# Convolution stage: the VectorE tap sums are built in PSUM, ScalarE and GpSimd take over one tap of each convolution, TensorE does two edge taps instead of three

## The reference

```
m = bilinear 32x32 -> 64x64 of mask
q, k, v = 1x1 convolutions of x; attention with 8 heads of 32 over the 4096 positions -> fuse
x = (Wf . [x, fuse] + bf) * m + x * (1 - m)                       # layer 0

edge = relu(bn(dwconv3x3(x, edge_w)))                             # nine taps for each channel
att  = sigmoid(fc2 . relu(fc1 . mean(x)))
out  = bn1(fusion_w . [x * att, edge] + fusion_b)
out  = dwconv3x3(out, deform_w)                                   # nine taps for each channel
out  = bn2(balance_w . out + balance_b)
return out * x                                                    # layer 1
```

## Time and profile before

| | |
|---|---|
| median of 3 executions | 4203.85 us (4203.06 to 4205.12) |
| the profiled execution | 4203.13 us, of which the span from first to last instruction is 4201.3 us |
| TensorE, busy share of the span | 96% |
| VectorE | 84% |
| GpSimd | 77% |
| ScalarE | 56% |
| granted TensorE clock, mean | 0.976 of full speed |

### The profile page before, as it was taken

One profiled execution on the slowest core, in us unless ns is written; L12 is line 12 of the kernel. 1 busy time (PEld: TensorE's weight loads), 2 busy tenths in 40 slices (PEclk: granted clock), 3 DMA queues, 4 the chain that ended last, 5 costly groups with the idle time before them and its releaser, 6 DMA issues. The chain is left out here.

```text
span 4201.3 us, 81722 instructions
## 1 busy us (share of the span) xinstructions
PE 4044.0 (96%) x20341; PEld 1975.3 (47%) x20341; DVE 3550.1 (84%) x5350; ACT 2339.9 (56%) x4424; POOL 3222.2 (77%) x1360
## 2 busy tenths in 40 slices
PE   7979999999999999999999999999999999969797
PEld 4534444444444444444444444444444444424343
DVE  3279999999989999999899999999999999917989
ACT  1216666666656666666566666666666666641213
POOL 2429999999989999999899999999999999960000
PEclk9959999999999999999999999999999999989998
DMA  6931100110001101110111011100110000013021
GB/s 190 285 100 39 41 21 22 42 39 22 21 23 41 31 21 32 41 31 21 31 41 31 21 31 38 35 20 18 40 38 21 21 21 21 17 27 85 20 80 40
DMA packets 213798, 184.92 MB, mean 44 GB/s; under 512 B 115986, under 2 KB 140740, under 8 KB 213316
## 3 DMA queue, kind: packets, MB, share of 16 engines
q1 hardware_dynamic: 213508, 181.74, 16.2%
HBM read 122.10 MB, written 59.24 MB: 43 GB/s over the span
## 5 line engine op out<-in xcount | busy, mean ns | idle before, releaser
L761 ACT ACTIVATE prob<-st 128x512 f32<-128x512 f32 x4096 | 2154.3, 601 | 1309.3 <-PE st L626 1048.6
L819 DVE TENSOR_REDUCE block_max<-mx 128x1 f32<-128x512 f32 x4096 | 2562.0, 683 | 343.4 <-PE mx L633 330.0
L490 POOL TENSOR_TENSOR prob_sum<-prob_sum,prob 128x1024 f32<-128x1024 f32 x768 | 1929.3, 2512 | 127.5 <-POOL prob_sum L490 100.4
L633 PE MATMUL mx<-keys,max_queries 96*128 96x512 f32 x4096 | 1648.0, 426 | 38.2 <-DMA keys<-k_scratch 27.8
L626 PE MATMUL st<-queries,keys 97*128 97x512 f32 x4096 | 1574.5, 411 | 1.6 <-ACT prob L761 1.5
L490 POOL TENSOR_TENSOR prob_sum<-prob 128x1024 f32<-128x1024 f32 x448 | 1067.8, 2383 | 253.1 <-ACT prob L761 253.1
L633 PEld LDWEIGHTS mx<-keys,max_queries 96*128 96x128 f32 x4096 | 777.8, 191 | 737.3 <-DVE block_max L819 564.8
L645 PE MATMUL acc<-prob,values 128*32 128x512 f32 x8192 | 1039.7, 602 | 0.0
L626 PEld LDWEIGHTS st<-queries,keys 97*128 97x128 f32 x4096 | 776.7, 190 | 520.6 <-ACT prob L761 282.2
L645 PEld LDWEIGHTS acc<-prob,values 128*32 128x32 f32 x8192 | 194.4, 108 | 427.1 <-issue 226.1
L665 PE MATMUL dacc<-prob_sum,ones 128*32 128x512 f32 x2048 | 273.0, 605 | 9.2 <-POOL prob_sum L490 9.2
(11 more groups left out here) (119 smaller groups left out, 1213.8 us busy)
## 6 DMA issues: line engine op xcount, KB each, us to landing
max_queries<-q_scratch SPq DMA_DIRECT2D x384, 64.0 KB, 1.9
queries<-q_scratch SPq DMA_DIRECT2D x384, 64.0 KB, 2.0
keys<-k_scratch SPq DMA_DIRECT2D x168, 128.0 KB, 2.5
x<-in_x SPq DMA_DIRECT2D x18, 512.0 KB, 4.1
q_scratch<-high SPq DMA_DIRECT2D x32, 256.0 KB, 4.4
k_scratch<-high SPq DMA_DIRECT2D x16, 512.0 KB, 4.9
q_scratch<-low SPq DMA_DIRECT2D x32, 256.0 KB, 5.0
k_scratch<-low SPq DMA_DIRECT2D x16, 512.0 KB, 4.9
```

What stands on the lines that cost most here:

```text
L490: ops.tensor_tensor(psum[k][:, :, :], a[:, :, :], prob[(first + i) % RING][:, :, :], ALU.add).then_inc(added[own], 1)
L633: nc.tensor.matmul(mx[bank(j, p)][:, :], qm[p][:, h, ns * P:(ns + 1) * P], kk[gp][0:SPLIT, h, blk * CH:(blk + 1) * CH], start=True, stop=T ...
L761: nc.scalar.activation(prob[s % RING][:, h, :], st[bank(i, p)][:, :], ACT.Exp).then_inc(exp_done, 1)
L819: nc.vector.tensor_reduce(bmax[p][:, j // MB, j % MB:j % MB + 1], mx[bank(j, p)][:, :], AX.X, ALU.max).then_inc(mx_taken, 1)
```

## The change

`EDGE_PE` goes from 3 to 2: TensorE does edge taps 0 and 1. VectorE does edge taps 2 to 7, in place in the PSUM tile `back[p][ct]`, and only its last step writes `conv[p]` in SBUF. The deform sum is built in the same way: ScalarE writes tap 0 into `back`, VectorE does taps 1 to 7 there (seven steps where there were eight), the last of them writing `conv`. For both convolutions ScalarE weighs tap 8 into a new SBUF tile `tap[p]` and GpSimd adds it to `conv[p]` (`add_tap`). The consumers of `conv` (`relu` on ScalarE, `balance` on TensorE) wait for GpSimd's sum. Since `back[p]` now holds the deform sum of a chunk as well as its balance product, ScalarE's deform taps wait for `last_ready`, and in ScalarE's order `balanced(c)` stands ahead of `deform_taps(c+2)`.

```
-EDGE_PE = 3
-EDGE_DVE = TAPS - EDGE_PE
-DEFORM_DVE = TAPS - 1
+EDGE_PE = 2
+EDGE_DVE = TAPS - EDGE_PE - 1
+DEFORM_DVE = TAPS - 2
...
+        tap = [sb(f"last_tap{p}", [P, CT, CH]) for p in range(2)]
...
 # TensorE: edges(), balance()
-                pe.wait_ge(edge_step, EARLIER * EDGE_DVE + CT * EDGE_DVE * (n - 2) + CT)
+                pe.wait_ge(edge_step, EDGE_DVE * (EARLIER + CT * (n - 1)))
...
-                pe.wait_ge(deform_step, CT * DEFORM_DVE * (n + 1))
+                pe.wait_ge(tap_added, CT * (deform_round(b, c) + 2))
...
 # ScalarE: relu(), and the taps
-                    act.wait_ge(edge_step, EDGE_DVE * (EARLIER + CT * (b * NCH + c)) + CT * (EDGE_DVE - 1) + ct + 1)
+                    act.wait_ge(tap_added, CT * (edge_round(b, c) + 1) + ct + 1)
...
+            def last_tap(src, weights, c, p, r):
+
+                act.wait_ge(tap_added, CT * r)
+                for ct in range(CT):
+                    nc.scalar.activation(as_rows(tap[p][:, ct, :]), inner(src, ct, c, k=TAPS - 1), ACT.Identity,
+                                         scale=keep[weights][:, ct, TAPS - 1:TAPS]).then_inc(tap_ready, 1)
+
+            def edge_tap(b, c, p, nxt=1):
+                act.wait_ge(y_ready, tile_done(b * NCH + c + nxt, CT - 1))
+                last_tap(y, "etaps", c, p, edge_round(b, c))
+
+            def deform_taps(b, c, p, nxt=1):
 
                 n = b * NCH + c
                 act.wait_ge(o1_ready, tile_done(n + nxt, CT - 1))
-                act.wait_ge(bal_mm, freed(n))
+                act.wait_ge(edge_step, EDGE_DVE * (EARLIER + CT * NCH * (b + 1)))
+                act.wait_ge(last_ready, freed(n))
                 for ct in range(CT):
-                    nc.scalar.activation(as_rows(conv[p][:, ct, :]), inner(o1, ct, c, k=0), ACT.Identity,
-                                         scale=keep["dtaps"][:, ct, 0:1]).then_inc(tap_ready, 1)
+                    nc.scalar.activation(as_rows(back[p][ct][:, :]), inner(o1, ct, c, k=0), ACT.Identity,
+                                         scale=keep["dtaps"][:, ct, 0:1]).then_inc(first_ready, 1)
+                last_tap(o1, "dtaps", c, p, deform_round(b, c))
...
 # ScalarE: order (each relu(c) has edge_tap(c + 1) ahead of it)
                         fused(b, c2 * 2 + p + 3, 1 - p)
-                        first_tap(b, c2 * 2 + p + 2, p)
                         balanced(b, c2 * 2 + p, p, c2)
+                        deform_taps(b, c2 * 2 + p + 2, p)
                 fused(b, NCH - 1, 1)
-                first_tap(b, NCH - 2, 0)
                 balanced(b, NCH - 4, 0, HALF - 2)
-                first_tap(b, NCH - 1, 1, nxt=0)
-                for c in range(NCH - 3, NCH):
+                deform_taps(b, NCH - 2, 0)
+                balanced(b, NCH - 3, 1, HALF - 2)
+                deform_taps(b, NCH - 1, 1, nxt=0)
+                for c in range(NCH - 2, NCH):
                     balanced(b, c, c % 2, c // 2)
...
 # GpSimd
+            def add_tap(p, r, step, done):
+
+                for ct in range(CT):
+                    pool.wait_ge(step, done + ct + 1)
+                    pool.wait_ge(tap_ready, CT * r + ct + 1)
+                    nc.gpsimd.tensor_tensor(conv[p][:, ct, :], conv[p][:, ct, :], tap[p][:, ct, :], ALU.add
+                                            ).then_inc(tap_added, 1)
...
 # VectorE: edges() and deform()
+                        part = as_rows(back[p][ct][:, :])
                         nc.vector.scalar_tensor_tensor(
-                            out=as_rows(conv[p][:, ct, :]), in0=inner(y, ct, c, k=k),
-                            scalar=keep["etaps"][:, ct, k:k + 1],
-                            in1=as_rows(back[p][ct][:, :] if i == 0 else conv[p][:, ct, :]),
+                            out=part if i < EDGE_DVE - 1 else as_rows(conv[p][:, ct, :]), in0=inner(y, ct, c, k=k),
+                            scalar=keep["etaps"][:, ct, k:k + 1], in1=part,
                             op0=ALU.mult, op1=ALU.add).then_inc(edge_step, 1)
...
                 dve.wait_ge(o1_ready, tile_done(n + nxt, CT - 1))
+                dve.wait_ge(edge_ready, tile_done(b * NCH + NCH - 2 + p, CT - 1))
+                dve.wait_ge(bal_mm, freed(n))
```

More of the change, by code:

```diff
@@ L915, in image_phase @@
         edge_step = sem("edge_step")
-        tap_ready = sem("first_tap_ready")
+        first_ready = sem("first_tap_ready")
+        tap_ready = sem("last_tap_ready")
+        tap_added = sem("last_tap_added")
         edge_ready = sem("edge_ready")
@@ L939, in image_phase @@
         tile_done = lambda n, t: EARLIER + CT * n + t + 1
+        edge_round = lambda b, c: 2 * NCH * b + c
+        deform_round = lambda b, c: 2 * NCH * b + NCH + c
         def inner(t, ot, c, rows=ROWS, k=4):
@@ L1118, in fused @@
                                          bias=keep["nshift"][:, 1, ot:ot + 1]).then_inc(o1_ready, 1)
-            def first_tap(b, c, p, nxt=1):
+            def last_tap(src, weights, c, p, r):
[7 more added lines that the diff above has]
+            def deform_taps(b, c, p, nxt=1):
                 n = b * NCH + c
                 act.wait_ge(o1_ready, tile_done(n + nxt, CT - 1))
-                act.wait_ge(bal_mm, freed(n))
+                act.wait_ge(edge_step, EDGE_DVE * (EARLIER + CT * NCH * (b + 1)))
+                act.wait_ge(last_ready, freed(n))
                 for ct in range(CT):
-                    nc.scalar.activation(as_rows(conv[p][:, ct, :]), inner(o1, ct, c, k=0), ACT.Identity,
-                                         scale=keep["dtaps"][:, ct, 0:1]).then_inc(tap_ready, 1)
+                    nc.scalar.activation(as_rows(back[p][ct][:, :]), inner(o1, ct, c, k=0), ACT.Identity,
+                                         scale=keep["dtaps"][:, ct, 0:1]).then_inc(first_ready, 1)
+                last_tap(o1, "dtaps", c, p, deform_round(b, c))
             def balanced(b, c, p, c2):
@@ L1139, in _ @@
                 act.sem_inc(s, EARLIER)
+            act.sem_inc(tap_added, CT)
             with act.Fori(0, B) as b:
+                edge_tap(b, 0, 0)
                 with act.Fori(0, HALF - 2) as c2:
                     for p in range(2):
+                        edge_tap(b, c2 * 2 + p + 1, 1 - p)
                         relu(b, c2 * 2 + p, p)
+                edge_tap(b, NCH - 3, 1)
                 relu(b, NCH - 4, 0)
@@ L1149, in _ @@
                 nc.scalar.activation(nexp[:, :], front[1][1][:, 0:CT], ACT.Exp, scale=-1.0).then_inc(nexp_ready, 1)
+                edge_tap(b, NCH - 2, 0)
                 relu(b, NCH - 3, 1)
+                edge_tap(b, NCH - 1, 1, nxt=0)
                 relu(b, NCH - 2, 0)
@@ L1154, in _ @@
                 fused(b, 1, 1)
-                first_tap(b, 0, 0)
+                deform_taps(b, 0, 0)
                 fused(b, 2, 0)
-                first_tap(b, 1, 1)
+                deform_taps(b, 1, 1)
                 with act.Fori(0, HALF - 2) as c2:
@@ L1174, in _ @@
                     nc.gpsimd.memset(edge_rows, 0.0).then_inc(borders, 1)
+            def add_tap(p, r, step, done):
[4 more added lines that the diff above has]
+                                            ).then_inc(tap_added, 1)
+            with pool.Fori(0, B) as b:
+                with pool.Fori(0, HALF) as c2:
+                    for p in range(2):
+                        c = c2 * 2 + p
+                        add_tap(p, edge_round(b, c), edge_step,
+                                EDGE_DVE * (EARLIER + CT * (b * NCH + c)) + CT * (EDGE_DVE - 1))
+                with pool.Fori(0, HALF) as c2:
+                    for p in range(2):
+                        c = c2 * 2 + p
+                        add_tap(p, deform_round(b, c), deform_step,
+                                CT * DEFORM_DVE * (b * NCH + c) + CT * (DEFORM_DVE - 1))
         @block.vector
@@ L1236, in deform @@
                         if i == 0:
-                            dve.wait_ge(tap_ready, CT * n + ct + 1)
+                            dve.wait_ge(first_ready, CT * n + ct + 1)
                         else:
                             dve.wait_ge(deform_step, base + CT * (i - 1) + ct + 1)
[L1240 to L1243, removed]
+                        part = as_rows(back[p][ct][:, :])
+                        nc.vector.scalar_tensor_tensor(
+                            out=part if i < DEFORM_DVE - 1 else as_rows(conv[p][:, ct, :]), in0=inner(o1, ct, c, k=i + 1),
+                            scalar=keep["dtaps"][:, ct, i + 1:i + 2], in1=part,
+                            op0=ALU.mult, op1=ALU.add).then_inc(deform_step, 1)
             def result(b, c, p):
```

## The result

The changed kernel takes 4233.08 us (median of 4, 4232.05 to 4238.42) beside 4203.45 us before (median of 4): a ratio of 1.0073, 95% interval 1.0055 to 1.0090, so 29.6 us slower. The forecast was 4230, slower.

The account below looks back on a forecast made before the run. TensorE was taken to pace the edge part, VectorE the deform part. 2 x (-4.1 - 5.3) + 7 x 6.0 + 1.2 + 1.9 = +26.3 us on 4203.13 gave 4229.4, for the median 4230; range 4206 to 4252.

Parts of the forecast that it names:

- The wait for the store: Deform loop: `balanced(c)` awaits the store of chunk c-2 ahead of the first tap, leaving VectorE idle 5.4 us a period.
- first reading: Kernel before: ScalarE's 106.4 us in ten waits on the store cost nothing, since VectorE never stands for them.
- The additions against VectorE: GpSimd's additions hold VectorE operations with both inputs in SBUF: result products 1.9 us a chunk, edge `y` 0.6.
- rival 2: Deform and edge parts: the additions don't hold VectorE's products and `y` operations; 23 us less, 4207; chance 8%.
- rival 4: Mainly the edge part: GpSimd also holds steps such as `diff`, because of their pointer scalar; +20 us, about 4250; chance 5%.
- The steps in PSUM: VectorE's edge and deform steps writing PSUM in place keep a spacing of 0.663 us from start to start.
- Rivals 1: VectorE's steps in PSUM don't overlap: +29 us, 4259; chance 14%.
- 3: VectorE's steps are shorter in PSUM: at 0.605 us spacing 20 us less, 4210; chance 9%.
- 5: VectorE's steps: write and read of one PSUM bank take turns, doubling the step; +187 us, 4417; chance 3%.
- rival 6: Deform loop: the chain over the store doesn't form, its wait being met early; 38 us less, 4192; chance 3%.
- The edge part: VectorE becomes the pace at 11.13 us a chunk; with the passage to the deform part, -4.1 us an image.
- The deform part and the end: Deforms 0 to 3 give -5.3 us an image; seven periods cost +6.0 each; image 1's rest +1.2, the end +1.9.

Follow-up runs that it names:

- experiment 3: The changed kernel with GpSimd adding only one of 512 columns of each last tap, all waits kept: 4206.25 us, 1.0010 of the kernel before.
- experiment 1: The changed kernel with `result(c)` ahead of `deform(c+3)` in VectorE's deform loop instead of behind it: 4193.17 us, 0.9978 of the kernel before.
- experiment 2: The changed kernel with four tiles `last` instead of two, VectorE's order kept: 4192.74 us, 0.9980 of the kernel before.
- experiment 5: The changed kernel with `result(c)` after the first two double steps of `deform(c+2)`, for chunks 0 to 5: 4181.88 us, 0.9956 of the kernel before.
- experiment 8: The changed kernel with the deform sum in SBUF (`conv`) and ScalarE's order as before the change: 4219.34 us, 1.0045 of the kernel before.
- experiment 4: The changed kernel with VectorE's sums in SBUF (`conv`), only each chunk's first step reading `back`: 4234.97 us, 1.0078 of the kernel before.
- experiment 6: experiment 5 plus edge steps placed between `diff` and `y` and ahead of the gate's operations: 4177.32 us, 0.9943 of the kernel before.

## Why the prediction was right, step by step

*The wait for the store.* Shown. Seven waits of 5.33 to 5.58 us where 5.4 was taken, and 38 to 40 us go with either of two edits that have only the store's wait in common.

The prediction's first reading went too far, though: it says that the wait costs nothing before the change and that VectorE never stands for it. That holds in the loop. At the passage between the images of the kernel before ScalarE waits 33.43 us for a store, and VectorE's results 6 and 7 wait 7.24 us for ScalarE (ScalarE's timeline, then VectorE's):

```profile
4003.59 2.79 ACT L1134 ACTIVATE last<-back,nshift,nscale 128x512 f32<-128x512 f32 x4 [33.43 <-DMA out_dram<-last]
...
4004.40 2.70 DVE L1248 TENSOR_TENSOR last<-last,y 128x512 f32<-128x512 f32 x4 [7.24 <-ACT last L1134]
```

After the change VectorE waits 7.46 us there, so the sum isn't touched.

*The additions against VectorE.* Shown in place and size: pairs of products of 3.09 to 3.16 us where 1.21 + 1.9 was forecast, `y` of 1.32 to 1.40 for 0.68 (at eleven places; rival 2 counts twelve), and 1.29 again for the products without the additions. `diff`, whose pointer scalar lies in SBUF, isn't held, which settles rival 4 at nothing. The Trainium skill (SBUF — State Buffer, Who interferes with whom) says that a VectorE instruction with two SBUF inputs contends with a GpSimd instruction that reads SBUF, and that one with at most one SBUF input doesn't, outside VectorE's 2-port modes; the trace agrees for these forms, with 3.09 for 1.29 and 1.40 for 1.40.

*The steps in PSUM.* 0.659 from start to start; 744 and 750 ns on average beside 745 and 746. Rivals 1, 3 and 5 fall; rival 2 falls with experiment 3, rival 6 with experiments 1 and 2. The Trainium skill's extra 65 ns for a PSUM source (VectorE: DVE Perf Modes, The TRN2 errata) doesn't show here either: 384 more steps have such a source, and the average of neither group is longer by more than 5 ns.

*The edge part.* The chunk was right (11.10 for 11.13), the stretch gained 2.0 and 2.4 us instead of 4.1. The mis-sized term is the gate, which the sum left out. It runs between edge chunks 5 and 6 and collides with the additions of chunk 5. VectorE's timeline, before and after:

```profile
3866.52 0.16 DVE L1221 TENSOR_SCALAR gate<-nexp 128x2 f32<-128x2 f32 x1
...
3866.91 0.62 DVE L1226 TENSOR_SCALAR fus<-fuT,gate 128x256 f32<-128x256 f32 x2
```

```profile
3858.07 0.90 DVE L1268 TENSOR_SCALAR gate<-nexp 128x2 f32<-128x2 f32 x1
...
3859.21 1.38 DVE L1273 TENSOR_SCALAR fus<-fuT,gate 128x256 f32<-128x256 f32 x2
```

That is 0.90 and 1.38 us for 0.16 and 0.62, 1.5 us more an image.

*The deform part and the end.* Between deform 0 and the mask 15.8 us were lost for 14.6: in image 1 TensorE waited 3.72 us for the first additions, and the balance product behind that took 5.36 us for 3.6, at a granted clock of 0.67 (3893.2 to 3898.3). Deforms 2 and 3 stood 0.15 and 1.03 us for what follows from it. The wait alone doesn't decide this: in experiments 1 and 2 TensorE waits 3.72 us at the same place and the product takes 3.67 (clock 1.00 in experiment 1), and in image 2 of the changed kernel it waits 2.21 us, the product takes 3.67, and no deform stands for it. The stretch of image 2 came out at 21.2 for 20.6.

The sum was 26.3, the image phase shows 31.8: 3.0 are the gate, 1.2 the small waits of deforms 2 and 3, and 1.3 are spread over the rest. Attention ended 3.0 us earlier in this execution, so the span grew by 28.8. The mechanism was right; that the time came out 3.1 us from the forecast, and not 5.5, is in part luck.

## What to carry to other kernels

When a tile takes on a second use, look at what its new release stands behind in the queue of the engine that refills it. Here a wait for which VectorE had never stood in the loop was put ahead of the first tap, and one exchange of two calls on another engine takes it out again. Work given to GpSimd costs VectorE as much as collides with its operations on two SBUF tiles; four steps with an input in PSUM between the release of the additions and the next such operation removed the cost (1.29 us for the products in experiment 5). The same change with both points seen to is 0.6% faster than the kernel before instead of 0.7% slower.

## What the hardware did that was not expected

*Who waits depends on what VectorE does back to back.* An addition that GpSimd has begun holds VectorE's operation with two SBUF inputs (1.29 us to 3.09 for a pair). An unbroken run of such operations holds GpSimd instead, for as long as it lasts: 9.7 us in experiment 8. In experiment 4 the same products, at the end of such a run, weren't held at all. Why the second addition gets in between two products when the first product was held, and doesn't between two that follow a run, wasn't tried.

*An operation on two columns is held too.* The gate's 128x2 operation has only one tensor input, in SBUF, and took 0.90 us beside 0.16. So counting SBUF inputs isn't enough to say what GpSimd holds. It takes 0.17 us again in experiment 6, where four steps stand ahead of it.

*ScalarE writes PSUM a little faster:* 682 ns for the first tap into `back`, beside 714 for the same tap of the same view into SBUF in the kernel before, and 707 for the last tap, another view of the same tile, into SBUF.
